# Last attention of a fused decoder layer: GpSimd's splitting of q and k in pieces between its other work, and the stores and loads of q and k moved into the queue of the softmax sums

## The reference, cut to what matters

```
x = x + self_attention_with_bias(layernorm(x))       # 16 heads of 8, B=8, S=256, D=128
h = layernorm(x)
h = self_output(cross_attention(h, ctx_1024), h)     # 1601 context rows, co_w, co_g, co_be
sa = _mha(h, h, None, sq_w, sq_b, sk_w, sk_b, sv_w, sv_b)   # the "last attention"
h = self_output(sa, h, so_w, ...); h = self_output(gelu(h @ fi_w), h, ...)
x = x + h
x = x + mixture_of_experts(layernorm(x))             # 8 experts, top 2
```

## Time and profile before

| | |
|---|---|
| median of 3 runs | 1246.9 us (1243.72 to 1254.9) |
| the profiled execution | 1246.21 us, of which the span in the trace is 1244.4 us |
| PE busy | 1062.8 us (85%) |
| DVE busy | 986.2 us (79%) |
| ACT busy | 855.6 us (69%) |
| POOL busy | 407.2 us (33%) |

### The profile page before, as it was taken

How to read it: one execution, slowest core, us unless ns; L and a number is a source line. 1 busy time by engine, 2 the same in 40 slices (tenths; PEclk the granted TensorE clock), 3 DMA queues, 4 the chain that set the end, 5 groups by cost and what they waited for, 6 DMA issues and landing times. The chain is left out here.

```text
span 1244.4 us, 32719 instructions
## 1 busy us (share of the span) xinstructions
PE 1062.8 (85%) x11548; PEld 580.2 (47%) x11548; DVE 986.2 (79%) x2786; ACT 855.6 (69%) x1759; POOL 407.2 (33%) x838
## 2 busy tenths in 40 slices
PE   5899966899999999999999999996778879349993
PEld 2455534344444444444444444443334446338883
DVE  7688846789889898898988989992689968766664
ACT  3599944387878878788788887883379855325553
POOL 4222214050140511404105041012533425736662
PEclk8799987699999999999999999998779989669997
DMA  6943036405232143321432204100462031201113
GB/s 190 213 96 68 24 85 153 123 28 129 70 76 67 33 123 76 74 69 33 120 79 64 79 7 117 30 2 7 121 135 70 15 114 51 85 13 46 48 46 119
DMA packets 90178, 96.35 MB, mean 77 GB/s; under 512 B 18569, under 2 KB 76337, under 8 KB 90018
## 3 DMA queue, kind: packets, MB, share of 16 engines
q1 hardware_dynamic: 85922, 87.96, 28.1%
q0 software_dynamic: 2496, 5.12, 1.5%
q10 hardware_dynamic: 1600, 1.18, 0.3%
HBM read 67.62 MB, written 27.82 MB: 77 GB/s over the span
## 5 line engine op out<-in xcount | busy, mean ns | idle before, releaser
L1616 DVE TENSOR_REDUCE MG<-bank 128x1 f32<-128x401 f32 (+1 forms) x1024 | 515.5, 566 | 69.3 <-PE bank L1395 67.7
L1535 ACT ACTIVATE PT<-bank 128x512 f32<-128x512 f32 (+1 forms) x624 | 334.1, 598 | 53.0 <-PE bank L1413 52.7
L1413 PE MATMUL bank<-QP,KP 54*128 54x256 bf16 (+1 forms) x1664 | 253.0, 273 | 10.9 <-ACT PT L1535 1.4
L1395 PE MATMUL bank<-KP,QP 54*128 54x401 bf16 (+1 forms) x1024 | 236.0, 343 | 9.8 <-DMA KP<-ctx_k_parts 4.6
L1433 PE MATMUL bank<-PT,VP 128*9 128x256 f32 (+1 forms) x2688 | 198.0, 367 | 0.8 <-ACT XT L1535 0.8
L1706 POOL TENSOR_TENSOR MP<-MN,ZERO 128x4 bf16<-128x4 f32 x128 | 26.4, 206 | 417.6 <-DVE MN L1623 412.6
L1413 PEld LDWEIGHTS bank<-QP,KP 54*128 54x128 bf16 (+1 forms) x1664 | 111.6, 96 | 100.6 <-ACT PT L1535 24.1
L1395 PEld LDWEIGHTS bank<-KP,QP 54*128 54x128 bf16 x1024 | 75.5, 93 | 119.6 <-DVE MG L1616 98.1
L1535 ACT ACTIVATE XT<-bank 128x512 f32<-128x512 f32 (+1 forms) x208 | 117.1, 599 | 19.9 <-PE bank L1413 19.5
L1040 PE MATMUL bank<-QP,KP 51*128 51x256 bf16 x512 | 91.2, 280 | 16.4 <-DVE MN L1152 7.9
L1433 PEld LDWEIGHTS bank<-PT,VP 128*9 128x9 f32 (+1 forms) x2688 | 76.3, 90 | 58.2 <-issue 21.3
(11 more groups left out here) (287 smaller groups left out, 1855.9 us busy)
## 6 DMA issues: line engine op xcount, KB each, us to landing
KP<-ctx_k_parts SPq DMA_DIRECT2D x128, 100.1 KB
ctx_k_parts<-KPARTS SPq DMA_DIRECT2D x16, 600.4 KB
KP<-ctx_k_parts SPq DMA_DIRECT2D x128, 50.0 KB
CN<-in_ctx SPq DMA_DIRECT2D x8, 768.0 KB
RAW<-in_w_gate_up SPq DMA_DIRECT2D x8, 512.0 KB, 3.8
QP<-q_parts SPq DMA_DIRECT2D x20, 192.0 KB
ctx_k_parts<-KPARTS SPq DMA_DIRECT2D x16, 200.1 KB
UQ<-bias_table SPq DMA_DIRECT2D x4, 768.0 KB, 7.2
```

The source lines that it names most:

```text
L1395: nc.tensor.matmul(GRAIN[n % NG][:, 0:w], k.QP[half, p, b * S + 128 * qt:b * S + 128 * (qt + 1)], k.KP[half, p, a:a + w], start=True, stop ...
L1413: return nc.tensor.matmul(bank[0:rows[t], S * at:S * (at + 1)], k.KP[half, p, 128 * t:128 * t + rows[t]], k.QP[half, p, b * S:(b + 1) * S] ...
L1535: nc.scalar.activation(PT[n % NP][0:rows[t], :], bank_of("s", g, t)[0:rows[t], :], ACT.Exp).then_inc(exp_done, 1)
L1616: nc.vector.tensor_reduce(MG[:, g % 4, 2 * s + qt, chunk:chunk + 1], GRAIN[n % NG][:, 0:w], AX.X, ALU.max).then_inc(m_read, 1)
```

## The change

POOL runs root 0 to 2, splits item 2 at once, then root 3, then splits item 3; its wait for done is gone. Items 4 to 7 are split later, one operation of the twelve after each split_maxima of units 2 to 13. SP stores and loads group 1 as before; the stores of group 2 stand behind place(0) and those of group 3 behind place(2). In batches 1 and 3, SP waits for stored[2] or stored[3] behind spread, issues the group's keys before give and its queries between give and place. (Items 4 to 7 have all been copied by ACT before the first unit starts.)

```
-        for g in range(4):
+        for g in range(3):
             root(k, pl, g, self.eps_added, self.rstd)
-        pl.wait_ge(self.done, 4)
-        for i in range(2, 8):
-            self.split_item(pl, nc.gpsimd, i)
+        self.split_item(pl, nc.gpsimd, 2)
+        root(k, pl, 3, self.eps_added, self.rstd)
+        self.split_item(pl, nc.gpsimd, 3)
+
+    def split_step(self, pl, n):
+        i, step = 4 + n // 3, n % 3
...
+        if step == 0:
+            pl.wait_ge(self.copied, i + 1)
+            ns.tensor_tensor(x, x, parts[0], ALU.subtract).then_inc(sem, 1)
+        elif step == 1:
+            pl.wait_ge(sem, base + 1)
+            ns.tensor_copy(parts[1], x).then_inc(sem, 1)
+        else:
+            pl.wait_ge(sem, base + 2)
+            ns.tensor_tensor(parts[2], x, parts[1], ALU.subtract).then_inc(sem, 1)
...
-        for c in range(1, 4):
-            self.store_item(sp, 2 * c)
-            self.store_item(sp, 2 * c + 1)
-            sp.wait_ge(self.stored[c], 64)
-            if c < 3:
-                load_keys(k, sp, 2, c, qk_in[c])
-                load_queries(k, sp, 2, c, qk_in[c])
+        self.store_item(sp, 2)
+        self.store_item(sp, 3)
+        sp.wait_ge(self.stored[1], 64)
+        load_keys(k, sp, 2, 1, qk_in[1])
+        load_queries(k, sp, 2, 1, qk_in[1])
         for b in range(LAST_BATCH):
             take(sp, b)
             spread(sp, b)
-            if b == 0:
-                load_keys(k, sp, 2, 3, qk_in[3], halves=(0,))
-            if b == 1:
-                load_keys(k, sp, 2, 3, qk_in[3], halves=(1,))
-            if b == 2:
-                load_queries(k, sp, 2, 3, qk_in[3])
+            c = 2 + b // 2 if b in (1, 3) else None
+            if c:
+                sp.wait_ge(self.stored[c], 64)
+                load_keys(k, sp, 2, c, qk_in[c])
             give(sp, b)
+            if c:
+                load_queries(k, sp, 2, c, qk_in[c])
             place(sp, b)
+            if b in (0, 2):
+                self.store_item(sp, 4 + b)
+                self.store_item(sp, 5 + b)
...
+                if not bias and 2 <= u < 14:
+                    front.split_step(pl, u - 2)
```

More of the change, by code:

```diff
@@ L792, in gpsimd @@
         nc.gpsimd.memset(k.VPS[:, :, :, HD:HD + 1], 1.0).then_inc(self.ones_set, 1)
-        for g in range(4):
+        for g in range(3):
             root(k, pl, g, self.eps_added, self.rstd)
-        pl.wait_ge(self.done, 4)
-        for i in range(2, 8):
-            self.split_item(pl, nc.gpsimd, i)
+        self.split_item(pl, nc.gpsimd, 2)
[3 more added lines that the diff above has]
+        i, step = 4 + n // 3, n % 3
+        what, c = self.ITEMS[i]
+        sem, base = self.split[1], 3 * (self.TURN[i] - 1)
+        x, slots = self.XF[:, i, :], SLOT_K if what == "k" else SLOT_Q
+        parts = [self.PARTS[:, int(what == "k"), slot, 512 * c:512 * (c + 1)] for slot in slots]
+        ns = self.k.nc.gpsimd
+        if step == 0:
[7 more added lines that the diff above has]
+            ns.tensor_tensor(parts[2], x, parts[1], ALU.subtract).then_inc(sem, 1)
     def prepare(self, i):
```

## The result

| | before | changed |
|---|---|---|
| median | 1248.33 us (4 runs, 1243.72 to 1254.9) | 1260.93 us (4 runs, 1257.15 to 1263.21) |
| ratio, 95% interval | | 1.0102 [1.0071, 1.0133] |
| the profiled execution, span | 1246.21, 1244.4 us | 1261.28, 1259.4 us |
| DVE busy | 986.2 us | 990.9 us |
| POOL busy | 407.2 us | 407.3 us |

The changed kernel is 12.6 us slower by the medians, 15.1 by the two profiled executions. The work is the same (DVE and POOL busy as before); DVE stands more. The prediction of 1250 (1243 to 1257) was too low.

What follows compares the result with a forecast made beforehand. DVE was taken to bound the phase, busy 19.57 of 20 us. From 1246.2 us: 3.5 gained at the front, 1.2 lost to blocked DVE, 0 for split steps, 6.2 lost to SP's order gave 1250.1, stated as 1250, range 1243 to 1257.

Steps and rivals of the forecast that it cites:

- Part 1: Phase start: POOL splits only items 2 and 3 before the first unit, so its first maxima operation starts 3.5 us earlier.
- Part 2: Front: POOL's splitting beside DVE's normalise blocks DVE in the two last groups; 1.2 us lost, bounds 0 and 2.0.
- DVE's first stood until POOL's was over: DVE's second normalise pass: its first operation waits out one large POOL operation, 2.14 us in place of 1.14, 1.0 per pass.
- some tenths more if they meet POOL's other two operations: Same passes: DVE's operations may lag some tenths of a us further beside the item's other two POOL operations.
- The cover that I had found: Last group's second pass: PE is still busy with the third group's projection, covering 1.1 us of its 2.0 us.
- Part 3: Units 2 to 13: twelve split operations fit POOL's idle time at cost 0, up to 12 x 0.3 us if not.
- Part 4: SP's order, batches 1 and 3: late REC stalls DVE 3.1 us per group (bounds 1.6 and 4.5), 6.2 us lost.
- the chain up to place: SP's issues in batch 1: give at 947.5, six query loads until 952.2, place at 952.3 in place of 949.2.
- REC lands behind the queries' data, at 952.2 + 2.7 + some 1.2 = 956.1: Batch 1: REC waits out 2.7 us of queued query data plus its own 1.2; DVE stands 3.0 us before scale(1).
- Rival B: Batches 1 and 3: PE's idling also drops its clock, 6.5 us per stall, sum 1256.9; chance 0.25.
- A: Rival, batches 1 and 3: loads fit the gaps, only the front counts, 1243.9 or 1242.7 us; chance 0.15.
- C: Rival, front: first unit waits for something else, so the change gains nothing measurable there, 1253.6 us; chance 0.05.

Runs made afterwards that it cites:

- experiment 3: Changed kernel, but of items 2 and 3 POOL runs only the first subtraction behind the root, the rest after DVE's second pass; 1254.43 us, a single execution.
- experiments 1 to 3: Three runs with SP's new order: POOL waiting for DVE's last normalise (1.0044), POOL splitting all six items first (1.0102), one POOL operation beside each pass (1254.43 us).
- experiment 7: Kernel before, with six query loads of group 2 between give and place of batch 1 alone and other loads of groups 2 and 3 moved; ratio 1.0024.
- experiment 4: Changed kernel, but in batches 1 and 3 place is issued before the six loads of queries; ratio 1.0137 to the kernel before.
- experiments 5 and 8: Both: POOL waits for DVE's last normalise, SP loads at most six per batch (0.9957); the second also stores item 7 behind place(1) (0.9982).
- experiment 1: Changed kernel, but POOL runs all four roots and waits for DVE's last normalise before splitting items 2 and 3; ratio 1.0044, median 1253.34 us.
- experiment 5: Changed kernel, with POOL waiting for DVE's last normalise and SP issuing six loads per batch, none between give and place; ratio 0.9957, median 1242.77 us.

## Why the prediction was wrong, step by step

**Part 1 was right.** 3.5 us from POOL's early start were forecast; L776 to the first copy shortened by 3.53, to where DVE's seven grains are the limit (they end at 907.11, the copy starts at 907.22).

**Part 2: the step that failed is "DVE's first stood until POOL's was over", taken as 1.0 us per pass.** The row it rested on the earlier trace rows has one large POOL operation; the change puts three in a row there. Three of DVE's four operations were held (3.40 us, 2.26 more than 1.14), with one held it is 2.02 (experiment 3), and of 2 x 2.26 = 4.5 us some 3.56 reached L776. Forecast 1.2, bounds 0 to 2.0; measured 3.56, outside them. For one operation per pass the forecast was about right (0.85 in experiment 3). What I called lagging "some tenths more if they meet POOL's other two operations" was the larger part. The cover that I had found, PE's projections, was worth 1.0, near the 1.1 counted. The prediction had the price of one blocked operation right, and then counted one of three.

**Part 3 was right:** nothing lost by the twelve steps (12.58 us per batch with them and without).

**Part 4: the chain up to place was right in batch 1** (give forecast 947.5, measured 947.30; place 952.3 and 952.47). **The step that failed is "REC lands behind the queries' data, at 952.2 + 2.7 + some 1.2 = 956.1".** It was usable at 958.4. From the first key load to REC that is 12.9 us forecast (943.2 to 956.1) and 15.6 measured; batch 3 has 14.7, and the six such batches of experiments 1 to 3 have 15.2 to 16.8. The 2.7 us of queue behind the last issue came from a batch with six loads, while here twelve follow each other, and the 1.2 us for REC's own way behind them rested on no row. With six loads (experiment 7) the same sum, 949.89 + 2.7 + 1.2 = 953.8, is short by 1.4 already (955.17); with twelve, in batch 1, by 2.4. There the 1.54 MB were issued in 9.2 us, 167 GB/s, and the DMA engines moved 139 GB/s between 944 and 954, so a backlog grew. In batch 3 the issuing slowed down to 147 GB/s (10.5 us) beside 151 moved: the sum behind the last issue held within 0.4 us (985.9 + 3.9 = 989.8, measured 990.12), and the term "six loads issued in 4.34 us" was short instead (5.04 and 4.76). The delay is that of the whole burst; where in the queue it shows differs. The same holds for the queries that PE waits for: 954.9 forecast, 958.5 measured. With that the waits for REC are 5.3 and 4.8 us, both above the upper bound of 4.5, and not 3.1. Experiment 4 shows that the prediction was right to count both waits: with REC's 3 us shorter, PE's is left, and it costs more.

**Rival B then came true as well.** PE stood for 5.6 us, the clock fell to 0.50 at 957, and the batches lost another 1.7 and 1.1 us behind the wait. That this is the clock's price is supported by experiments 5 and 8 (0.94 beyond the wait with the fall, nothing without); up to 0.43 of the 1.7 is DVE's next wait for PE. B had only 0.25. Its 6.5 us per group is near the measured 7.06 and 5.87, in part by luck, since its stall of 4.5 was too short and its 2.0 for the clock too long. With it and the measured front the sum is 1246.2 + 0 + 13.0 = 1259.2, near the median of 1260.9; my figure for B, 1256.9, had the front 2.3 us too good. A and C are refuted, A by the two waits, C by experiment 1. Also wrong was that 1% is about what a measurement can tell from no change: the 1.0% here has an interval of 0.3% on either side.

Two prices that I read from the nearest row, one POOL operation and one batch of loads, were each off because the change puts several of the same kind in a row. The median leaves the stated range (1243 to 1257) by 3.9 us: 3.56 - 1.2 = 2.4 from the front and 12.9 - 6.2 = 6.7 from the two batches are the terms that were short, and 2.0 behind the phase were in no term.

## What to carry to other kernels

When a row of the trace shows one operation blocking or one burst queued, and the change puts three operations or two bursts in a row, multiply before you bound. A small DMA on the critical chain is late behind any bulk load still in flight; putting it ahead in the queue moves the lateness to the loads if these are wanted too (experiment 4), and smaller bursts, well before either is wanted, helped here (experiment 5). A gap in the issuing queue is no gap in the transfers. Work moved to an idle engine may be better started after the neighbour that it would block has finished, even if that engine then waits: here that was worth 2.7 to 3.6 us.

## What the runs showed of the hardware that I had not expected

VectorE's operations with two SBUF inputs were held by GpSimd's large ones, one by each: beside three that took 1.15, 0.61 and 1.15 us, as long as without VectorE beside them, VectorE's took 1.24, 0.75 and 1.31 us, and the fourth, with GpSimd done, 0.34. The Trainium skill, page "SBUF — State Buffer", section "SBUF: two separate sides", speaks of an exclusive lock for a whole instruction; the trace agrees, and shows four short operations against three long ones paying three waits and not one.

A load of 128 KB issued behind six loads of 768 KB in all was usable 5.2 us after its issue, behind twelve 4.1 to 7.0 (eight batches), against a median of 2.4; 16 KB stored behind six loads took 3.7 and 4.9 us (experiment 4) against 1.4 to 2.4 in batches 1 to 5 of the kernel before.

TensorE's clock in the stretch ahead of the phase was at 0.50 during the last projections in some kernels and at 1.00 in others, with the same work there (3.78 and 1.98 us). That moves L776 by 2 us, and the first unit too where POOL is no longer the limit (root 2 to the first copy 21.09 in experiment 1). What decides it was not tried.
